# A graph network kernel: GpSimd waits once for each pair of edge groups, not for each group

## The chip, the cores and the metric

One core of a Trainium2 chip runs the whole kernel. The metric is the time of one execution on the device in microseconds (us). The kernel before was run three times: 3107.74, 3111.16 and 3117.75 us, with a median of 3111.16 us.

## What is computed

Four graph layers run over the same graph of 3125 nodes and 53125 directed edges; a layer's output is added to its input and normalised. Features are 128 wide, in float32.

```python
x = _layernorm(x + _L0_gnn_ref(x, edge_index, edge_type_4, ...), axis=-1)     # relation layer
x = _layernorm(x + _L1_gnn_ref(x, edge_index, edge_attr_64, ...), axis=-1)    # messages
x = _layernorm(x + _L2_gnn_ref(x, ..., node_type_3, src, dst), axis=-1)       # attention heads
x = _layernorm(x + _L3_gnn_ref(x, edge_weight, src, dst), axis=-1)            # weighted sum
```

The relation layer, for each of 4 relation types:

```python
rel_in = jnp.concatenate([node_features[src], node_features[tgt]], axis=1)
rel_t = _lrelu(rel_in @ W_R[r] + b_R[r])
...
e = _lrelu(jnp.concatenate([Q, K], axis=1) @ a_w + a_b)[:, 0]
attn = ex / jnp.maximum(denom[tgt], 1e-16)
h = h + jax.ops.segment_sum(V * attn[:, None], tgt, num_segments=num_nodes)
```

The attention layer computes a score for 8 heads of 16 features for every edge, a softmax over the edges of one destination, and a weighted sum. The last layer is `segment_sum(vals[:, None] * x[cols], rows)`: here the rows are the sources, while the edges lie in the order of their destinations.

## The kernel before

**Groups.** The edges are cut into Q = 104 groups of 512, a group into J = 4 tiles of 128 edges, one edge on each partition. Thirteen groups make a chunk of the softmax. Nodes are worked on in NG = 5 blocks of 640.

**Passes.** After tables are laid out (0 to 97 us of the trace), four passes go over the 104 groups, one behind the other: the relation pass (97 to 816 us), the message pass (935 to 1640 us), the head pass (1678 to 2325 us) and the scatter pass (2325 to 2968 us). A last pass over the nodes (2968 us to the end) reads what the scatter pass has written. The node work of a pass is woven into its later turns.

**Programs.** Each engine has its own program, written out as a list of turns; the engines meet at semaphores. `hold(engine, semaphore, n)` is a wait for the semaphore to reach n, and nothing when n is 0 or less.

**Relation pass.** In turn q, SyncE (`load`) brings the keys of the group (L710) and 4 small windows of the destination table (L715), for which it waits on `expanded` of two groups before and on `parted_keys`. ScalarE makes a one-hot `spread` of the keys (`spread_made`). TensorE (`expand`, L754) multiplies spread by window, so that each edge has its destination's row in PSUM (3 buffers), and counts `expanded`. GpSimd (`pool_program`, L690 to L697) gathers the source rows with one indirect DMA for each tile (L696) into one of GS = 6 buffers `gathered`. VectorE adds both (`join`, L988), applies the leaky ReLU (L992), and multiplies (L997); ScalarE sums (L897, `reduced`). TensorE adds up a group 21 turns later (L769 to L771).

**Head pass.** It has the same shape: loads L1899 and L1909, `expand` at L1955, gathers of 4 x 128 rows at L1867 into a ring of RING = 24 groups `kv`, `score` on VectorE (L2231, L2234), which reads them, and much later `weigh` (L2240, `weighed`), which frees the ring's slot. At the start of the pass SyncE also loads the links of the first chunk (L1891).

**Scatter pass.** `weigh_row(q)` (VectorE, L2169, `taken`) waits for `expanded` of its group and writes edge weight times node row into a slot of the same ring. `tag(q)` (ScalarE, L2106, `tagged`) adds a column with the source. `mark` and `place` (VectorE, L2176 to L2197, with TensorE's `count`, L1968 to L1970) find, for two groups at a time, in which row of `rows_by_src` each edge belongs (`placed`). GpSimd (`send_rows`) writes the rows with one indirect DMA for each tile (L1881). `number[True, q]` is the place of scatter group q in the order of expansions, and for the text below E(q) is the expansion of scatter group q. In this order `weigh_row(q)` waits for E(q), while `send_rows` before the change waits for E(q + 1) as well.

Instructions of one engine start in program order, so an unmet wait on GpSimd holds every indirect DMA behind it.

Of the kernel before, what the change touches and what calls it, by code (L numbers as in the profile page):

```python
# [32 lines left out]
Q = -(-E // GE)  # L33
# [21 lines left out]
RING = 2 * CH  # L55
# [11 lines left out]
def build(nc, x, src, dst, edge_attr_64, edge_type_4, edge_weight, node_type_3,  # L67
# [340 lines left out]
    def far_spread(eng, program):  # L408

        reach = nc.values_load(wide[0:1, 3:4], engines=[eng.engine], min_val=0, max_val=GE,  # L410
                               skip_runtime_bounds_check_because="every node has an edge of its own")
        with eng.If(reach < REACH):
            program(1, REACH, True)
        with eng.Else():
            program(GE // P, P, False)
# [6 lines left out]
    def hold(eng, semaphore, count):  # L422

        if not (isinstance(count, int) and count <= 0):
            eng.wait_ge(semaphore, count)
# [183 lines left out]
    def rel_layer(u_cols, agg, share, parts):  # L609

        with ExitStack() as ctx:
            tmp, psum, sem, pair = scope(ctx, "e0")
            GS, SLOTS, WS, KS, SS, AHEAD = 6, CH + 8, 3, 2, 2, CH + 8
# [50 lines left out]
            spread_made, expanded, joined, shaped, scaled, reduced = (sem(n) for n in  # L664
                ("spread_made", "expanded", "joined", "shaped", "scaled", "reduced"))
# [23 lines left out]

            def pool_program(pool):  # L690
                for q in range(Q):
                    hold(pool, reduced, q - GS + 1)
                    hold(pool, expanded, q)
                    pool.nop(nofuse=True)
                    for j in range(J):
                        pool.indirect_dma_start(gathered[:, q % GS, j, :], None, rel_table,  # L696
                                                bass.IndirectOffsetOnAxis(ap=rel_idx[:, q * J + j:q * J + j + 1], axis=0)).then_inc(src_in[q % GS], 16)  # L697
# [534 lines left out]
            with nc.Block() as block:  # L1232
                @block.gpsimd
                def _(pool):
                    pool_program(pool)

                @block.sync
                def _(sp):
                    tiles_and_spread(sp, lambda nw, early: sync_program(sp, nw, early))

                @block.tensor
                def _(pe):
                    tiles_and_spread(pe, lambda nw, early: pe_program(pe, nw, early))

                @block.scalar
                def _(act):
                    tiles_and_spread(act, lambda nw, early: act_program(act, nw, early))

                @block.vector
                def _(dve):  # L1250
                    tiles_and_spread(dve, lambda nw, early: dve_program(dve, nw, early))
# [462 lines left out]
    def head_and_rows(agg2, parts, below, bucket, first_bucket, bucket_base):  # L1714

        with ExitStack() as ctx:
            tmp, psum, sem, pair = scope(ctx, "e2")
            ROWS = CH * H
            RING, WS = 24, 3
# [70 lines left out]
            prepared, bucketed, scanned, carried, counted, chosen, ranked, placed, tagged, starts_mm, starts_out, based = (sem(n) for n in  # L1790
                ("prepared", "bucketed", "scanned", "carried", "counted", "chosen", "ranked", "placed", "tagged", "starts_mm", "starts_out", "based"))
            SAID, BASES = 4, 4 * (Q // PIECE)
            links_in = sem("links_in")
            distant, spread_made, expanded, taken, reduced, weighed, marked, marked_far, summed, parted, added = (sem(n) for n in
                ("distant", "spread_made", "expanded", "taken", "reduced", "weighed", "marked", "marked_far", "summed", "parted", "added"))
# [38 lines left out]
            def numbers(early):  # L1834

                return {which: n for n, which in enumerate(x for t in range(first_row(early) + Q) for x in expansions(t, early))}
# [23 lines left out]

            def pool_program(pool):
                for q in range(Q):
                    hold(pool, weighed, q - RING + 1)
                    hold(pool, expanded, q - 4)
                    pool.nop(nofuse=True)
                    for j in range(J):
                        pool.indirect_dma_start(kv[:, q % RING, j, :], None, kv_table,  # L1867
                                                bass.IndirectOffsetOnAxis(ap=src_idx[:, q * J + j:q * J + j + 1], axis=0)).then_inc(src_in[q % RING], 16)
                far_spread(pool, lambda nw, gw, early: send_rows(pool, early))

            def send_rows(pool, early):
                number = numbers(early)
                for q in range(Q):
                    slot = (Q + q) % RING
                    pool.wait_ge(taken, number[True, q] + 1)
                    pool.wait_ge(expanded, number[True, min(q + 1, Q - 1)] + 1)
                    pool.wait_ge(tagged, q + 1)
                    pool.wait_ge(placed, q // 2 + 1)
                    pool.nop(nofuse=True)
                    for j in range(J):  # L1880
                        pool.indirect_dma_start(in_order, bass.IndirectOffsetOnAxis(ap=row[:, q // 2 % RS, q % 2 * J + j:q % 2 * J + j + 1], axis=0),  # L1881
                                                kv[:, slot, j, 0:D + 1], None).then_inc(sent[slot], 16)
                for slot in range(RING):
                    pool.wait_ge(sent[slot], 16 * J * len([q for q in range(Q) if (Q + q) % RING == slot]))
# [641 lines left out]
            with nc.Block() as block:  # L2526
                @block.gpsimd
                def _(pool):
                    pool_program(pool)

                @block.sync
                def _(sp):
                    far_spread(sp, lambda nw, gw, early: sync_program(sp, nw, gw, early))

                @block.tensor
                def _(pe):
                    far_spread(pe, lambda nw, gw, early: pe_program(pe, nw, gw, early))

                @block.scalar
                def _(act):  # L2540
                    far_spread(act, lambda nw, gw, early: act_program(act, nw, gw, early))

                @block.vector
                def _(dve):
                    far_spread(dve, lambda nw, gw, early: dve_program(dve, nw, gw, early))
# [259 lines left out]
```

## Time and profile before

| what | us |
|---|---|
| median of three runs | 3111.16 |
| lowest and highest run | 3107.74 and 3117.75 |
| span of the profiled execution | 3116.5 |
| GpSimd busy in it | 1686.7 |
| TensorE busy in it | 2083.1 |
| VectorE busy in it | 1599.0 |
| ScalarE busy in it | 1173.8 |

The profile is of one execution of its own. Its span, from first to last instruction, is 3116.5 us, which is 5.3 us above the median of the runs; no other time is recorded for that execution. An engine's idle time in front of an instruction is shown with what ended it. "issue" stands for time in which the profile sees no other engine that released it; a wait that was put on a semaphore ahead of an instruction on GpSimd can be counted there. The ends of matmuls are modelled. The shares of busy time hide that the passes have different limits, so the stretches are read one by one.

### The profile page before, as it was taken

To read this page: it belongs to the slowest core of one execution; us is meant where nothing else is said; L and a number is where in the kernel's file an instruction comes from. 1 tells how busy PE (TensorE), PEld (TensorE's weight loads), DVE (VectorE), ACT (ScalarE), POOL (GpSimd) and SP (SyncE) were. 2 spreads that over 40 slices of the span, in tenths; PEclk is the share of its full clock that TensorE was granted. 3 is DMA by queue.
4 is the path that set the end of the run, shared out by engine and by line. 5 is a ranking of instruction groups with operands and counts; after the bars stand their busy time and mean duration, and the time that the engine had idled before them with its cause. 6 is when DMAs were issued, how large, how long until landed. Compare 5 with 4: busy or idle time off the path is not lost. (4 is left out here: it accounts for less than half of the span.)

```text
span 3116.5 us, 39457 instructions
## 1 busy us (share of the span) xinstructions
PE 2083.1 (67%) x9935; PEld 1681.0 (54%) x9935; DVE 1599.0 (51%) x4408; ACT 1173.8 (38%) x3329; POOL 1686.7 (54%) x1704
## 2 busy tenths in 40 slices
PE   5336787878764778888883356766776665455367
PEld 2235666766653666667662356565664443333267
DVE  4246767786751233423232334666687754544256
ACT  2245556555321223233231234454454322222144
POOL 3366656565105566656623666666646666666600
PEclk9655555556556899899995555555567775655589
DMA  6644434443103223232312444444432222222265
GB/s 222 233 140 130 129 107 135 121 128 113 37 9 99 65 70 81 71 82 66 83 51 72 125 119 121 120 121 119 128 100 65 77 78 69 73 70 71 65 198 178
DMA packets 244613, 322.43 MB, mean 103 GB/s; under 512 B 105346, under 2 KB 160931, under 8 KB 243045
## 3 DMA queue, kind: packets, MB, share of 16 engines
q0 software_dynamic: 66560, 163.90, 18.3%
q1 hardware_dynamic: 177797, 155.67, 16.6%
q8 instruction: 93, 1.52, 0.2%
q14 instruction: 163, 1.34, 0.1%
HBM read 257.60 MB, written 63.38 MB: 103 GB/s over the span
## 5 line engine op out<-in xcount | busy, mean ns | idle before, releaser
L1318 POOL DMA_INDIRECT e_gathered<-msg_src_table,src_idx x416 | 399.9, 961 | 393.7 <-POOLq L364 142.1
L696 POOL DMA_INDIRECT e_gathered<-rel_src_table,rel_idx x416 | 427.9, 1029 | 310.2 <-issue 256.3
L1867 POOL DMA_INDIRECT e_kv<-kv_table,src_idx x416 | 411.1, 988 | 302.8 <-issue 198.9
L1881 POOL DMA_INDIRECT rows_by_src<-e_kv,e_row x416 | 422.2, 1015 | 226.4 <-issue 193.5
L1955 PE MATMUL e_ps_q<-e_window,e_spread 64*128 64x128 f32 x1664 | 347.6, 374 | 145.4 <-issue 61.3
L1955 PEld LDWEIGHTS e_ps_q<-e_window,e_spread 64*128 64x128 f32 x1664 | 302.3, 271 | 218.6 <-issue 187.7
L2092 ACT ACTIVATE e_spread<-e_offsets,e_minus_lane 64x512 f32<-64x512 f32 x208 | 149.1, 717 | 576.0 <-remote 370.0
L754 PE MATMUL e_ps_r<-e_window,e_spread 64*128 64x128 f32 x832 | 205.5, 421 | 156.4 <-DMA e_window<-rel_dst_table 117.6
L754 PEld LDWEIGHTS e_ps_r<-e_window,e_spread 64*128 64x128 f32 x832 | 176.7, 311 | 182.9 <-DMA e_window<-rel_dst_table 126.0
L1991 PE MATMUL e_ps_a<-e_onehot,e_weighted 128*128 128x128 f32 (+1 forms) x832 | 184.3, 394 | 127.6 <-DVE e_weighted L2240 85.4
L1581 DVE TENSOR_TENSOR e_shifted<-e_ps_m,e_b 128x512 f32<-128x512 f32 x104 | 71.8, 690 | 344.6 <-remote 169.6
L1991 PEld LDWEIGHTS e_ps_a<-e_onehot,e_weighted 128*128 128x128 f32 x832 | 165.6, 296 | 153.2 <-DVE e_weighted L2240 99.3
L769 PE MATMUL e_ps_a<-e_typed,e_rel 128*128 128x128 f32 (+1 forms) x832 | 192.1, 407 | 48.2 <-DVE e_typed L1005 30.7
L1968 PE MATMUL e_ps_c<-e_inside,e_minus_after 128*128 128x392 f32 x104 | 77.1, 841 | 205.1 <-DVE e_carry L2185 76.6
L769 PEld LDWEIGHTS e_ps_a<-e_typed,e_rel 128*128 128x128 f32 x832 | 174.1, 309 | 69.7 <-DVE e_typed L1005 36.3
L1425 PE MATMUL e_ps_a<-e_mixed,e_message 128*128 128x64 f32 x832 | 113.8, 282 | 83.8 <-DVE agg L1590 60.3
L897 ACT ACTIVATE e_gathered<-e_gathered 128x128 f32<-128x128 f32 x416 | 122.8, 296 | 122.7 <-issue 70.3
L1409 PEld LDWEIGHTS e_ps_h<-ident,e_gathered 128*128 128x128 f32 x832 | 127.7, 220 | 60.5 <-issue 60.5
L2099 ACT ACTIVATE e_onehot<-marks,part_t 128x66 f32<-128x66 f32 x416 | 110.1, 335 | 123.7 <-remote 99.2
L1425 PEld LDWEIGHTS e_ps_a<-e_mixed,e_message 128*128 128x128 f32 x832 | 107.1, 201 | 90.6 <-issue 89.8
L1504 ACT ACTIVATE e_hidden<-e_ps_h,e_b 128x512 f32<-128x512 f32 x104 | 71.4, 687 | 222.6 <-remote 116.6
L1404 PE MATMUL e_ps_h<-e_rhs,e_lhs 128*128 128x512 f32 x208 | 128.5, 704 | 36.7 <-issue 24.3
(446 smaller groups left out, 4233.3 us busy)
## 6 DMA issues: line engine op xcount, KB each, us to landing
n_rows<-rows_by_src SPq DMA_DIRECT2D x26, 1032.0 KB
e_offsets<-group_offsets SPq DMA_DIRECT2D x208, 128.0 KB
e_keys<-tile_keys SPq DMA_DIRECT2D x104, 128.0 KB
e_window<-rel_dst_table SPq DMA_DIRECT2D x416, 32.0 KB
e_mixed<-in_edge_attr_dram SPq DMA_DIRECT2D x103, 128.0 KB
rel_src_table<-t_up SPq DMA_DIRECT2D x5, 2560.0 KB
e_gathered<-rel_src_table,rel_idx POOLq DMA_INDIRECT x416
e_gathered<-msg_src_table,src_idx POOLq DMA_INDIRECT x416
```

The source lines that it names most:

```text
L696: pool.indirect_dma_start(gathered[:, q % GS, j, :], None, rel_table, bass.IndirectOffsetOnAxis(ap=rel_idx[:, q * J + j:q * J + j + 1], ax ...
L754: mm = pe.matmul(ps_r[q % 3][:, j, :], spread[:, at % SS, j * P:(j + 1) * P], window[:, at % WS, j, :], start=(w == 0 and (nw == 1 or j == ...
L769: pe.matmul(ps_a[at % 2][:, a:b], rel[:, p % SLOTS, j, :], by_key[:, a:b], start=True, stop=True, skip_group_check=True)
L1318: pool.indirect_dma_start(gathered[:, q % GS, j, :], None, msg_table, bass.IndirectOffsetOnAxis(ap=src_idx[:, q * J + j:q * J + j + 1], ax ...
L1404: pe.matmul(ps_h[q % 2][:, :, :], lhs[0:k, at % WS, :], rhs[0:k, at % 2, :], start=(w == 0), stop=False, skip_group_check=True).then_inc(s ...
L1409: mm = pe.matmul(ps_h[q % 2][:, j, :], gathered[:, q % GS, j, :], ident[:, :], start=False, stop=True, skip_group_check=True)
L1425: mm = pe.matmul(ps_a[:, :], message[:, q % 2, j, :], picked, start=(j == 0), stop=(j == J - 1))
L1867: pool.indirect_dma_start(kv[:, q % RING, j, :], None, kv_table, bass.IndirectOffsetOnAxis(ap=src_idx[:, q * J + j:q * J + j + 1], axis=0) ...
L1881: pool.indirect_dma_start(in_order, bass.IndirectOffsetOnAxis(ap=row[:, q // 2 % RS, q % 2 * J + j:q % 2 * J + j + 1], axis=0), kv[:, slot ...
L1955: mm = pe.matmul(ps_q[n % 2][:, j, :], spread[0:gw, at % 2, j * P:(j + 1) * P], window[0:gw, at % WS, :], start=(w == 0 and (nw == 1 or j ...
L1991: mm = pe.matmul(to[:, 0:n], weighted[:, p % 2, j, :], wide_hot[:, j * (gw + 2):j * (gw + 2) + n], start=(j == 0), stop=(j == J - 1), skip ...
L2092: act.activation(spread[0:gw, at % 2, :], offsets[0:gw, n % WS, :], ACT.Abs, bias=minus_lane[0:gw, w:w + 1]).then_inc(distant, 1)
```

## The change

In the relation and head passes, GpSimd's two waits (and the empty instruction that carries them) stand ahead of even groups only. The first wait asks for one group more, since the eight DMAs behind it fill two buffers. The second, for `expanded`, keeps its even value, so odd groups start with no wait of their own. In the scatter pass the four waits also stand ahead of even groups only, and ask for what the odd group needed: `taken` and `tagged` of both groups, and E(q + 2) for an even q. The message pass is as before. The number of indirect DMAs, their order and their data are the same.

```diff
--- before.py
+++ after.py
@@ -689,9 +689,10 @@
 
             def pool_program(pool):
                 for q in range(Q):
-                    hold(pool, reduced, q - GS + 1)
-                    hold(pool, expanded, q)
-                    pool.nop(nofuse=True)
+                    if q % 2 == 0:
+                        hold(pool, reduced, q - GS + 2)
+                        hold(pool, expanded, q)
+                        pool.nop(nofuse=True)
                     for j in range(J):
                         pool.indirect_dma_start(gathered[:, q % GS, j, :], None, rel_table,
                                                 bass.IndirectOffsetOnAxis(ap=rel_idx[:, q * J + j:q * J + j + 1], axis=0)).then_inc(src_in[q % GS], 16)
@@ -1860,9 +1861,10 @@
 
             def pool_program(pool):
                 for q in range(Q):
-                    hold(pool, weighed, q - RING + 1)
-                    hold(pool, expanded, q - 4)
-                    pool.nop(nofuse=True)
+                    if q % 2 == 0:
+                        hold(pool, weighed, q - RING + 2)
+                        hold(pool, expanded, q - 4)
+                        pool.nop(nofuse=True)
                     for j in range(J):
                         pool.indirect_dma_start(kv[:, q % RING, j, :], None, kv_table,
                                                 bass.IndirectOffsetOnAxis(ap=src_idx[:, q * J + j:q * J + j + 1], axis=0)).then_inc(src_in[q % RING], 16)
@@ -1872,11 +1874,12 @@
                 number = numbers(early)
                 for q in range(Q):
                     slot = (Q + q) % RING
-                    pool.wait_ge(taken, number[True, q] + 1)
-                    pool.wait_ge(expanded, number[True, min(q + 1, Q - 1)] + 1)
-                    pool.wait_ge(tagged, q + 1)
-                    pool.wait_ge(placed, q // 2 + 1)
-                    pool.nop(nofuse=True)
+                    if q % 2 == 0:
+                        pool.wait_ge(taken, number[True, q + 1] + 1)
+                        pool.wait_ge(expanded, number[True, min(q + 2, Q - 1)] + 1)
+                        pool.wait_ge(tagged, q + 2)
+                        pool.wait_ge(placed, q // 2 + 1)
+                        pool.nop(nofuse=True)
                     for j in range(J):
                         pool.indirect_dma_start(in_order, bass.IndirectOffsetOnAxis(ap=row[:, q // 2 % RS, q % 2 * J + j:q % 2 * J + j + 1], axis=0),
                                                 kv[:, slot, j, 0:D + 1], None).then_inc(sent[slot], 16)
```

## Rows read from the trace of the kernel before

**Rows 1.** Busy us by stretch: PE, PEld, DVE, ACT, POOL; PEclk, DMA share.
```profile
97.00:816.00 719.00, 495.30 (x2128) 421.42 (x2129) 476.00 (x1445) 385.26 (x1528) 427.86 (x416) 0.54 0.44 127
...
2325.00:2968.00 643.00, 360.99 (x1323) 241.06 (x1321) 334.87 (x751) 178.28 (x415) 422.19 (x416) 0.64 0.24 71
...
106.00:250.00 144.00, 54.22 (x218) 46.25 (x218) 58.39 (x101) 61.40 (x232) 92.92 (x92) 0.50 0.50 142
```

**Rows 2.** The waits of GpSimd by line (us in total, times, longest us).
```profile
POOL e_gathered L696 <- issue: 256.3, 412, 5.9
POOL e_kv L1867 <- issue: 198.9, 406, 4.1
POOL rows_by_src L1881 <- issue: 193.5, 402, 4.0
```

**Rows 3.** The waits of all engines by line: VectorE for gathers, TensorE for windows.
```profile
PE e_ps_r L754 <- DMA e_window<-rel_dst_table: 117.6, 24, 21.8
...
DVE e_rel L988 <- DMA e_gathered<-rel_src_table,rel_idx: 47.2, 13, 5.9
```

**Rows 4.** The chain that ended last, where the last pass begins (start, us, what).
```profile
2972.61 5.18 DMA n_rows<-rows_by_src
```

**Rows 5.** Timeline of GpSimd, start of the relation pass (last: idle before).
```profile
110.15 0.95 POOL L696 DMA_INDIRECT e_gathered<-rel_src_table,rel_idx  x1 [0.30 <-issue]
118.00 0.94 POOL L696 DMA_INDIRECT e_gathered<-rel_src_table,rel_idx  x1 [6.90 <-PE e_ps_r L754]
...
137.24 0.94 POOL L696 DMA_INDIRECT e_gathered<-rel_src_table,rel_idx  x1 [3.62 <-PE e_ps_r L754]
```

**Rows 6.** Timeline of SyncE in that stretch, the loads of four windows.
```profile
118.12 2.45 SPq L715 DMA_DIRECT2D e_window<-rel_dst_table  x4
...
125.55 8.63 SPq L715 DMA_DIRECT2D e_window<-rel_dst_table  x4
```

**Rows 7.** Timeline of TensorE and VectorE in that stretch.
```profile
134.41 2.08 PE L754 MATMUL e_ps_r<-e_window,e_spread 64*128 64x128 f32 x8 [9.71 <-DMA e_window<-rel_dst_table]
...
136.52 0.69 DVE L988 TENSOR_TENSOR e_rel<-e_gathered,e_ps_r 128x512 f32<-128x512 f32 x1 [4.24 <-PE e_ps_r L754]
```

**Rows 8.** Timeline late in the relation pass: eight gathers, loads beside them.
```profile
663.29 0.94 POOL L696 DMA_INDIRECT e_gathered<-rel_src_table,rel_idx  x1 [1.37 <-issue]
...
672.54 0.95 POOL L696 DMA_INDIRECT e_gathered<-rel_src_table,rel_idx  x1 [0.30 <-issue]
...
668.55 6.99 SPq L715 DMA_DIRECT2D e_window<-rel_dst_table  x4
...
681.83 1.43 PE L754 MATMUL e_ps_r<-e_window,e_spread 64*128 64x128 f32 x5
```

**Rows 9.** Timeline at the start of the head pass, SyncE and VectorE.
```profile
1686.83 7.14 SPq L1891 DMA_DIRECT2D e_pen_c<-segment_gates  x8
...
1703.21 0.69 DVE L2231 TENSOR_TENSOR e_kv<-e_kv,e_ps_q 128x512 f32<-128x512 f32 x1 [11.90 <-remote]
```

**Rows 10.** Timeline of GpSimd, scatter pass: starts of runs of DMAs.
```profile
2602.15 1.36 POOL L1881 DMA_INDIRECT rows_by_src<-e_kv,e_row  x1 [3.43 <-issue]
...
2626.38 1.29 POOL L1881 DMA_INDIRECT rows_by_src<-e_kv,e_row  x1 [3.36 <-issue]
...
2812.51 1.08 POOL L1881 DMA_INDIRECT rows_by_src<-e_kv,e_row  x1 [1.82 <-issue]
...
2836.90 1.09 POOL L1881 DMA_INDIRECT rows_by_src<-e_kv,e_row  x1 [1.69 <-issue]
```

**Rows 11.** Timeline at the end of the scatter pass, VectorE and GpSimd.
```profile
2908.66 0.69 DVE L2169 TENSOR_TENSOR e_kv<-e_ps_q,w_t 128x512 f32<-128x512 f32 x1 [2.29 <-remote]
...
2909.38 0.97 POOL L1881 DMA_INDIRECT rows_by_src<-e_kv,e_row  x1 [0.97 <-issue]
...
2916.84 0.96 POOL L1881 DMA_INDIRECT rows_by_src<-e_kv,e_row  x1 [2.67 <-issue]
...
2956.32 0.97 POOL L1881 DMA_INDIRECT rows_by_src<-e_kv,e_row  x1 [0.30 <-issue]
```

## Prediction

> **What bounds the kernel now.** I first read the busy time by stretch. No engine is full in any pass that the change touches: the relation pass lasts 719 us with TensorE busy 495, VectorE 476 and GpSimd 428, and the scatter pass lasts 643 us with GpSimd busy 422 and TensorE 361 [rows 1]. So a pass is set by waits between engines, and what counts is who waits for GpSimd.
>
> Next come the waits by line. GpSimd's own idle time is large: 256, 199 and 194 us in the three changed lines [rows 2]. It doesn't matter by itself. It matters where somebody waits for the DMAs behind it. In the relation pass VectorE's join waits for gathers 13 times, 47.2 us in all, while TensorE waits for its windows 24 times, 117.6 us [rows 3]. In the head pass the view shows VectorE's score waiting for a gather once, and in the scatter pass nobody waits inside the pass for a row that was written. At its end somebody does: the chain that ended last goes through the load of those rows at 2972.61 [rows 4], which can't begin before the last write.
>
> Then the timelines. A gather takes 0.95 us, and behind one whose wait is already met 0.30 us pass, between groups as within them. A wait that binds costs more: group 0's last gather starts at 110.15, and group 1's first only at 118.00, after 6.90 us for its expansion [rows 5]. In the stretch from 106 to 250 us (groups 0 to 23) nothing is left to do from earlier groups; GpSimd is busy for 92.9 of 144 us there, TensorE for 54 [rows 1]. Here the gathers are close to the bound. Later a gather has usually landed some microseconds before its join.
>
> One more reading decides much of what follows. SyncE's load of four windows takes 2.45 us at 118.12, when GpSimd has just started, but 8.63 us at 125.55, when GpSimd has issued DMAs back to back since 118.00 [rows 6]. TensorE's multiplication waits 9.71 us for that load, the join behind it starts at 136.52, and GpSimd itself then starts at 137.24, 3.62 us idle, for the expansion before it [rows 7, 5]. Late in the relation pass it is the same: GpSimd issues eight gathers in a row from 663.29 to 673.5, and the load at 668.55 takes 6.99 us [rows 8]. At the start of the head pass, with a longer run of gathers, a load of eight small pieces takes 7.14 us, and a score comes 11.90 us after VectorE's last work [rows 9]. So a long run of indirect DMAs is not free for the others.
>
> **The change part by part.**
>
> *The waits taken away that were met already.* Fifty-two waits of a pass fewer, each worth nothing: the gap behind a met wait is the same 0.30 us as within a group [rows 5]. Term: 0.
>
> *Relation pass, the opening.* Odd groups lose their wait for their own expansion. Group 1 then starts at about 111.4 (110.15 + 0.95 + 0.30) in place of 118.00, 6.6 us earlier. The other odd waits before group 24 add up by my reading of the same timeline to about 6, so 13 us is the most that the opening can give, if each gather is the last thing its join waits for. It gives nothing if windows come last. Group 1 is gathered earlier, but groups 2 and 3 then form a run of eight as before, and the window of group 3 is loaded beside it, as now at 125.55; that load, not a gather, holds the join at 136.52 [rows 6, 7]. What GpSimd gains ahead of that point is taken back there. I take -3, nearer to the window's row; bounds -13 and 0.
>
> *Relation pass, the rest.* Idle ahead of L696 put to "issue" is 256.3 us over 412 gathers [rows 2]; 412 x 0.30 = 123.6 is the plain gap, so 132.7 us stand at binding boundaries. The two shown in the rows are 3.62 and 1.37 [rows 5, 8], 2.2 above the gap in the mean, hence some 60 boundaries, half of them odd. So about 30 times two runs of four gathers (5 us) become one of eight (10 us). The odd gather comes earlier, for a join that mostly has another input last; but the load of windows that falls into the second half of the run can take 6.99 or 8.63 us instead of 2.45. The load at 668.55 ended at 675.54 and was used only at 681.83 [rows 8], 6.3 us later: it cost nothing. The one at 125.55 cost what it was late. Bounds: below 0; above, one in four of 30 pairs with the whole 6.2 us (8.63 - 2.45), 46 us. I take +4, two thirds of one such load, because after the opening SyncE is as a rule a group ahead.
>
> *Relation pass, the tighter wait for `reduced`.* It asks for q - 4 rather than q - 5; the expansion of q waits for the join of q - 3, a group later in VectorE's order, and ScalarE's sum of q - 4 follows its own join by a few us. It is met before the other wait. Term 0; above, one ScalarE group late on occasion, inside the +46.
>
> *Head pass.* Gathers are far ahead of the score (the ring has 24 groups, and only once does a score wait for one), and GpSimd already runs in long stretches. Neither the slot asked for earlier nor the odd gathers' earlier start meets anybody. If that cover were gone, the even group would wait one VectorE turn, some 5 us. The long run at its start [rows 9] has no binding odd wait in it and stays. Term 0, bounds 0 and +5.
>
> *Scatter pass, the body.* Odd groups' waits stay as they were in substance; even groups wait one expansion and one `weigh_row` longer. What matters is whether lumps of eight slow the pass. The trace has both forms: in runs of sixteen DMAs, four groups take 2626.38 - 2602.15 = 24.23 us; in runs of four to eight, 2836.90 - 2812.51 = 24.39 us [rows 10]. The pace is the same, so it is set by TensorE and VectorE, not by how GpSimd is fed. The slots, 24 groups, and the six pairs of row numbers hide the delay of one group. Term 0.
>
> *Scatter pass, the end.* Here there is no cover. Group 95 starts at 2909.38, 0.72 us after VectorE takes up expansion 96 at 2908.66; group 96 at 2916.84 after 2.67 us idle, and from there 32 writes run back to back to 2956.32 + 0.97 [rows 11]. With the pair, groups 94 and 95 both wait for that expansion: they start at 2909.4, eight writes take 8 x 1.27 = 10.2 us and 0.3 for a first one that is longer, and group 96 starts at 2919.9. That is 3.1 us later, and each write behind it, and the load of the last pass that waits for them all. Bounds: 0, if 96's own wait moves earlier, and +5.1, a whole group; I take +3.
>
> *A rule beside the rows.* By the rows, a window load beside a run of gathers goes from 2.45 to 8.63 us [rows 6]. The Trainium skill (DMA: Bandwidth & Descriptors, section "Issuing engines are not separate DMA queues") says that DMAs started by different engines run on the same 16 DMA engines and interleave, and that issuing from several saves only issue time. By it, lumping the same gathers would cost SyncE no more than its share of the same engines, and the +4 would be 0; the trace disagrees, since SyncE's issue itself is stretched.
>
> *The sum.* 0 - 3 + 4 + 0 + 0 + 3 = +4 us on the span of 3116.5, 3120.5 us. The median of the runs stands at 0.9983 of that span (3111.16 / 3116.5), so 3115 us.
>
> **The rivals.**
>
> *The opening decides, faster.* The 47.2 us that VectorE waited for gathers [rows 3] are mostly in the opening, and 6.9 us of it come from one odd wait [rows 5]. If the gathers are what bounds groups 0 to 23, and SyncE gets its loads out before a run grows long, all 13 us return: 3116.5 - 13 + 3 = 3106.5, or 3101 as a median, and more if the same holds in later places (another 10: 3091). Against it is the join at 136.52, bound by a window.
>
> *Longer runs starve the window loads, slower.* If one in eight of the 30 new runs of eight puts its full 6.2 us on TensorE, that is +23; with the tail's 3 and no gain in the opening, 3142.5, or 3137 as a median. It decides once four or so of those loads come late. For it: TensorE already waits 117.6 us for windows [rows 3], and 8.63 us is measured. Against: the load of 6.99 us that hurt nobody [rows 8].
>
> *Nothing of it is felt.* Each expansion is due before GpSimd gets there, or the joins have another input last: 0 everywhere but the tail, and that too may be taken by the work that goes on beside it. 3111.
>
> **How the numbers follow.** My forecast (a few us) has a chance of 0.32 and no effect 0.10, together 0.42 for within 0.3%, about 9 us, which is what a measurement of this kernel can tell from no change. Faster has 0.26: two shown places speak for it, one against. Slower has 0.32: it has many places in which to happen, and the tail's sign is certain. The range is 3090 (the opening's gain and more) to 3138 (one load in eight late); beyond it I leave 0.2, mostly above. The likeliest case's own range is 3105 to 3122.
>
> **What the profile after would show.** The step on the opening is right if group 1's gathers start near 111 and the join of group 3 is still held by a window; wrong if VectorE's waits for gathers fall by 10 us or more and the pass ends earlier. The step on the rest is right if TensorE's waits for windows stay near 118 us, and wrong if they grow by 20 or more while loads of 6 to 9 us multiply. In the scatter pass the pace should stay at 24.2 to 24.4 us for four groups, and the distance from `weigh_row` of group 96 to the last write should grow from 48.6 us (2908.66 to 2957.29) to about 52. What would make it wrong most easily: that the start of one pass moves, by chance, into another pattern of runs, since several patterns stand side by side in this trace, and each turn's start depends on the one before.

## The result, and the profile after

The changed kernel takes 3154.78 us (median of 4 runs, 3149.52 to 3165.36), the kernel before 3109.45 us (4 runs) beside it. The ratio is 1.0134, with a 95% interval of 1.0105 to 1.0163: 1.3% slower, some 42 us, where I had forecast a span 4 us longer.

The profiled execution has a span of 3157.5 us, 41.0 above the one before. The busy time by stretch, for the relation, head and scatter passes of the changed kernel (columns as in [rows 1]):

```profile
97.00:841.00 744.00, 488.39 (x2139) 414.63 (x2139) 478.17 (x1449) 386.86 (x1534) 425.66 (x416) 0.55 0.42 123
...
1705.00:2339.00 634.00, 375.75 (x1576) 324.20 (x1576) 338.77 (x803) 265.36 (x644) 408.35 (x416) 0.54 0.42 120
...
2368.00:3000.00 632.00, 346.35 (x1286) 231.79 (x1285) 327.74 (x735) 172.57 (x399) 425.57 (x416) 0.65 0.24 71
```

From the first indirect DMA of one pass to that of the next, which I worked out from the starts in the timelines, the relation pass with its node turns and the way to the message pass took 861.7 us in place of 837.1, the message pass 737.3 in place of 737.6, the head pass 662.7 in place of 648.9, and the writes of the scatter pass 629.4 in place of 626.5. Of the head pass's 13.8 us, 3.9 lie between its first gather and the end of its last (631.7 in place of 627.8); the other 9.9 lie in the wait ahead of the first write, which is 31.0 us in place of 21.1. No engine is busy for longer over the whole execution than before by more than 0.5 us, so the loss is made of waits.

The waits by line, of the changed kernel (us in total, times, longest):

```profile
POOL e_gathered L697 <- issue: 282.2, 413, 13.7
...
PE e_ps_r L755 <- DMA e_window<-rel_dst_table: 85.6, 19, 22.4
...
POOL rows_by_src L1884 <- DVE e_kv L2172: 80.5, 15, 31.0
...
DVE e_rel L989 <- DMA e_gathered<-rel_src_table,rel_idx: 41.7, 14, 5.5
```

and, of the kernel before, the wait ahead of the first write:

```profile
POOL rows_by_src L1881 <- DVE e_row L2197: 21.1, 1, 21.1
```

Against [rows 2, 3], VectorE's waits for gathers fell by 5.5 us and TensorE's for windows by 32. Neither is the place of the loss. GpSimd's longest wait in the relation pass went from 5.9 to 13.7 us. In the scatter pass 80.5 us of its idle time are now put to VectorE, but that is mostly another name for waits that stood under "issue" before: all its idle time there rose from 226.4 to 235.8 us, by no more than the wait ahead of the first write did. In the relation pass the thirty odd waits that had bound are gone, with 71 us of idle time in them, while the idle time at even groups rose from 68 to 157 us (both beyond the plain gaps). GpSimd comes sooner and is held longer, since the engines that feed it are late. To see why, one has to go to a long wait.

The opening of the relation pass in the changed kernel, GpSimd, SyncE and VectorE:

```profile
112.30 0.94 POOL L697 DMA_INDIRECT e_gathered<-rel_src_table,rel_idx  x1 [0.30 <-issue]
...
123.32 0.94 POOL L697 DMA_INDIRECT e_gathered<-rel_src_table,rel_idx  x1 [6.31 <-PE e_ps_r L755]
...
126.72 2.46 SPq L716 DMA_DIRECT2D e_window<-rel_dst_table  x4
...
130.44 4.41 SPq L716 DMA_DIRECT2D e_window<-rel_dst_table  x4
...
118.83 0.69 DVE L989 TENSOR_TENSOR e_rel<-e_gathered,e_ps_r 128x512 f32<-128x512 f32 x1 [9.25 <-PE e_ps_r L755]
...
135.27 0.69 DVE L989 TENSOR_TENSOR e_rel<-e_gathered,e_ps_r 128x512 f32<-128x512 f32 x1 [2.68 <-DMA e_gathered<-rel_src_table,rel_idx]
```

Group 1 is now gathered from 112.30, its join came earlier, and the join of group 3 at 135.27 is 1.3 us earlier than at 136.52 [rows 7], and waits for its gather and not, as I had it, for a window. Up to group 18 nearly all joins lie ahead of their times before, by up to 3.8 us, and the next ten lie on either side. That is about the gain of 3 us that I had put down. From about group 29 on the pass falls back, 10 us behind by group 44, and 24 by group 76, in steps. One step, in which group 67 loses 10 us:

```profile
550.35 0.94 POOL L697 DMA_INDIRECT e_gathered<-rel_src_table,rel_idx  x1 [2.11 <-issue]
...
569.75 0.95 POOL L697 DMA_INDIRECT e_gathered<-rel_src_table,rel_idx  x1 [0.31 <-issue]
584.41 1.15 POOL L697 DMA_INDIRECT e_gathered<-rel_src_table,rel_idx  x1 [13.71 <-issue]
...
552.19 5.26 SPq L716 DMA_DIRECT2D e_window<-rel_dst_table  x4
...
561.12 10.03 SPq L716 DMA_DIRECT2D e_window<-rel_dst_table  x4
...
577.69 2.45 SPq L716 DMA_DIRECT2D e_window<-rel_dst_table  x4
...
555.42 1.98 PE L770 MATMUL e_ps_a<-e_typed,e_rel 128*128 128x128 f32 x8
...
564.79 0.37 PE L770 MATMUL e_ps_a<-e_typed,e_rel 128*128 128x128 f32 x1 [1.18 <-issue]
566.95 0.37 PE L770 MATMUL e_ps_a<-e_typed,e_rel 128*128 128x128 f32 x1 [1.79 <-issue]
569.05 0.37 PE L770 MATMUL e_ps_a<-e_typed,e_rel 128*128 128x128 f32 x1 [1.73 <-issue]
571.19 0.37 PE L770 MATMUL e_ps_a<-e_typed,e_rel 128*128 128x128 f32 x1 [1.76 <-issue]
...
573.51 0.69 DVE L989 TENSOR_TENSOR e_rel<-e_gathered,e_ps_r 128x512 f32<-128x512 f32 x1 [11.21 <-remote]
```

GpSimd starts at 550.35 and issues sixteen gathers without a break, to 570.7: two pairs have run together. The load of four windows at 552.19 takes 5.26 us, the next one at 561.12 10.03 us, the first one after the run 3.34, and the second 2.45 again. TensorE shows the same: its pieces of work stood eight in 1.98 us at 555.42, but from 564.79 to 571.19 one matmul starts every 2.1 us, with nothing named that it waits for ("issue"). VectorE gets its expansion after 11.21 us, when the run is over, and GpSimd has then to wait 13.71 us itself. That a long run stretches a load beside it I had seen [rows 6, 8, 9]; that TensorE's own instructions crawl as well I had not priced.

### The profile page after: what moved, and what is told of

It is laid out like the page before. It is cut to its first block and busy times, and to the rows that moved or that the text cites. A ratio compares the mean times of both kernels' runs of the same rounds, so it can differ in the third digit from the quotient of the medians.

```text
span 3157.5 us, 39251 instructions
## 1 busy us (share of the span) xinstructions
PE 2060.7 (65%) x9935; PEld 1666.1 (53%) x9935; DVE 1598.8 (51%) x4408; ACT 1174.3 (37%) x3329; POOL 1683.6 (53%) x1704
## 5 line engine op out<-in xcount | busy, mean ns | idle before, releaser
L1884 POOL DMA_INDIRECT rows_by_src<-e_kv,e_row x416 | 425.6, 1023 | 235.8 <-issue 144.8
L1958 PE MATMUL e_ps_q<-e_window,e_spread 64*128 64x128 f32 x1664 | 336.0, 367 | 130.3 <-issue 61.5
L1958 PEld LDWEIGHTS e_ps_q<-e_window,e_spread 64*128 64x128 f32 x1664 | 294.5, 266 | 200.2 <-issue 182.4
L1405 PE MATMUL e_ps_h<-e_rhs,e_lhs 128*128 128x512 f32 x208 | 131.6, 719 | 42.5 <-issue 24.2
L989 DVE TENSOR_TENSOR e_rel<-e_gathered,e_ps_r 128x512 f32<-128x512 f32 x104 | 70.9, 682 | 172.0 <-remote 54.1
```

Of the source, the lines that this page charges most:

```text
L1405: pe.matmul(ps_h[q % 2][:, :, :], lhs[0:k, at % WS, :], rhs[0:k, at % 2, :], start=(w == 0), stop=False, skip_group_check=True).then_inc(s ...
L1958: mm = pe.matmul(ps_q[n % 2][:, j, :], spread[0:gw, at % 2, j * P:(j + 1) * P], window[0:gw, at % WS, :], start=(w == 0 and (nw == 1 or j ...
```

## The experiments

All ratios are to the kernel before on the same chip. In this section "theory A" is that unbroken runs of GpSimd's indirect DMAs stretch the other engines' instructions, that is, make them take longer, and that the change makes such runs longer. A run is counted as unbroken while no gap in it is over 0.5 us. The first four ran together.

**One pass at a time.** Relation pass alone:

```diff
                 for q in range(Q):
-                    hold(pool, reduced, q - GS + 1)
-                    hold(pool, expanded, q)
-                    pool.nop(nofuse=True)
+                    if q % 2 == 0:
+                        hold(pool, reduced, q - GS + 2)
+                        hold(pool, expanded, q)
+                        pool.nop(nofuse=True)
```

> The waits in pairs in the relation pass alone; head and scatter passes as before. Theory A (runs of eight and sixteen gathers stretch SyncE's window loads and TensorE's instructions, and the relation pass carries most of the loss): 20 to 30 us slower than before, the message pass starting 20 to 27 us later. Theory B (the loss is spread over the passes as a shift of patterns): under 10 us slower.

The same with the diff's head part alone, and with its scatter part alone:

> The waits in pairs in the head pass alone. Theory A: 0 to 10 us slower, since GpSimd runs long there with either form. Theory B, and that the tighter slot or the lumps matter in the head pass: 10 to 20 us slower, with the scatter pass starting later by as much.

> The waits in pairs in the scatter pass alone. Prediction: pace unchanged and the last write 3 us later relative to the last expansions, so 3 us slower. Theory C (the first pair waits for an expansion that comes late, as the scatter pass started 10 us later in the changed kernel's trace): 8 to 15 us slower.

Measured: 1.0075 (1.0047 to 1.0103) for the relation pass, 1.0039 (1.0019 to 1.0060) for the head pass, 1.0048 (1.0024 to 1.0072) for the scatter pass. On a median of 3138.54 us that is 24, 12 and 15 us. Each part costs by itself, and the three add up to 1.6%, which the intervals allow beside 1.34%. The head pass cost more than the 5 us that the prediction allowed it at most, and more than the 10 us that theory A did here; the scatter pass cost five times the 3 us that I gave it, which is theory C's band of 8 to 15. For the relation pass the 24 us lie in theory A's band, but its second sign didn't show: the message pass started at 958.4 us, against 951.2 to 954.4 in the other three traces of this chip, and not 20 to 27 us later. (Its profiled execution is one of its faster ones, 3150.18 us beside a median of 3163.79.)

Theory C's late first pair is there, but it isn't the cost. From the end of the last gather to the first write it is 26.3 us in the trace with the scatter pass in pairs and 21 to 25 us in traces with the head and scatter passes as before. It is 26.0 us as well in the version "late, but not in a lump" below, which isn't slower.

**The run broken, all else kept.** GpSimd fills a small buffer ahead of each odd group:

```diff
                     if q % 2 == 0:
...
+                    else:
+                        for i in range(3):
+                            hold(pool, rested, q // 2 * 3 + i)
+                            pool.memset(rest[:, :], 0.0).then_inc(rested, 1)
+                        pool.wait_ge(rested, q // 2 * 3 + 3)
+                        pool.nop(nofuse=True)
```

> The relation pass in pairs, but ahead of each odd group GpSimd fills a small buffer three times (each waiting for the one before), so that eight gathers are never issued back to back; other passes as before. The fills compute nothing. Theory A: the loss of the relation pass goes, 0 to 8 us slower than before. Theory B, or that the tighter wait or the earlier odd gathers do it: as slow as with the relation pass in pairs alone, within 5 us.

Its GpSimd timeline at a group boundary:

```profile
302.22 1.09 POOL L704 DMA_INDIRECT e_gathered<-rel_src_table,rel_idx  x1 [0.30 <-issue]
303.31 0.74 POOL L700 MEMSET e_rest<- 128x128 f32 x3
304.81 1.92 POOL L704 DMA_INDIRECT e_gathered<-rel_src_table,rel_idx  x1 [0.75 <-issue]
```

The gap between the last gather of one group and the first of the next is 1.50 us (304.81 - 303.31) in place of 0.30, and 1.49 to 1.66 at all 52 odd groups; the odd group still starts without its old wait, and the even one has the tighter wait for `reduced`. Measured: 1.0002 (0.9980 to 1.0024), against 1.0075 without the rest on the same chip. The loss is gone, though GpSimd needs 1.2 us more for each pair. So the moved wait costs nothing. The rest does two things at once, it breaks the run and it brings the odd gathers 1.2 us later, and this run doesn't part the two; that the break is what helps is read from SyncE's loads further below.

**The rest in all three passes** (in the head and scatter passes one fill, a gap of 0.9 us), on another chip with the next three:

> The changed kernel with a rest of GpSimd ahead of each odd group in all three passes: three fills of a small buffer in the relation pass (the gap grows from 0.30 to 1.8 us there), one fill in the head and scatter passes (a gap of about 1 us). The fills compute nothing. Theory A (unbroken runs of indirect DMAs do the harm, in all three passes): within 8 us of before. Theory D (in head and scatter the lump of eight or the later even group does it, not the unbroken run): 15 to 30 us slower than before, as the two passes cost alone.

Measured 1.0038 (1.0012 to 1.0063), 12 us, which lies between theory A's band and theory D's, with an interval that reaches into both. It is less than the changed kernel in both its measurements (1.0134, and 1.0107 with an interval of 1.0069 to 1.0145 below), so most of the loss comes back, not all. The remainder isn't a matter of run length: with the rests no run in the three passes is longer than eight DMAs, where the kernel before has runs of up to 32. From the first gather of the head pass to the first write, its trace has 653.9 us, against 662.7 to 667.6 in the three traces with that pass in pairs without a rest, and 643.4 to 657.4 in the nine with it as before. In its trace the last write starts 64.6 us after `weigh_row` 96, in that of before 47.7; the four rests in that stretch explain some 2 us of it, and the remainder isn't traced.

**Late, but not in a lump.** In the scatter pass each group keeps a wait, for one group more:

```diff
-                    pool.wait_ge(taken, number[True, q] + 1)
-                    pool.wait_ge(expanded, number[True, min(q + 1, Q - 1)] + 1)
-                    pool.wait_ge(tagged, q + 1)
+                    pool.wait_ge(taken, number[True, min(q + 1, Q - 1)] + 1)
+                    pool.wait_ge(expanded, number[True, min(q + 2, Q - 1)] + 1)
+                    pool.wait_ge(tagged, min(q + 2, Q))
```

> Scatter pass only: every group keeps a wait of its own, but asks for one group more (weigh_row and tag of q + 1, E(q + 2)), so that writes are as late as the even ones of the pairs and are not lumped. Theory A: the lumps cost, so only the tail's 3 to 6 us remain. Theory E (the later even group costs, since it holds ring slots and row numbers longer, or since the last writes come later): 10 to 18 us slower.

Measured 1.0003 (0.9981 to 1.0024). The later wait of the even groups, the one price that I had put into the scatter pass, costs nothing that can be measured; 3 us would lie inside the interval. What is left for the 0.48% of the scatter pass in pairs is the lump of eight. That is by elimination, and between two chips: the two intervals meet at 1.0024.

**More breaks than before.** The kernel before with one fill ahead of odd groups in the head and scatter passes:

> The kernel before, with one fill of a small buffer on GpSimd ahead of odd groups in the head and scatter passes, which breaks its runs of 16 to 32 DMAs. Theory A: since the kernel before has such runs itself, 5 to 20 us faster. Rival: TensorE and VectorE set the pace there, and the longer GpSimd turn eats what is won; within 0.3%.

Measured 1.0007 (0.9986 to 1.0027). No run was longer than eight DMAs there, and nothing was won: theory A missed as far as it said that all long runs cost. The head and scatter passes of before live with the runs that they have.

**The dose.** One wait for four groups in the relation pass:

```diff
+                    if q % 4 == 0:
+                        hold(pool, reduced, q - GS + 4)
+                        hold(pool, expanded, q)
+                        pool.nop(nofuse=True)
```

> Relation pass only: one wait ahead of sixteen gathers, for four groups. Theory A: the longer the run, the longer window loads are stretched: at least 45 us slower, twice the loss of the pairs. Theory B (a pattern, not a dose): about the same 20 to 25 us, or less.

Measured 1.0436 (1.0408 to 1.0464), 136 us. Its timelines of GpSimd, SyncE and VectorE show a run of sixteen:

```profile
402.95 1.13 POOL L697 DMA_INDIRECT e_gathered<-rel_src_table,rel_idx  x1 [9.65 <-PE e_ps_r L755]
...
432.93 0.95 POOL L697 DMA_INDIRECT e_gathered<-rel_src_table,rel_idx  x1 [9.71 <-ACT e_gathered L898]
...
408.87 6.56 SPq L716 DMA_DIRECT2D e_window<-rel_dst_table  x4
...
422.62 0.69 DVE L989 TENSOR_TENSOR e_rel<-e_gathered,e_ps_r 128x512 f32<-128x512 f32 x1 [14.18 <-remote]
```

The run goes from 402.95 to 423.2, the load at 408.87 takes 6.56 us, and a join comes after 14.18 us. There are 22 such runs of sixteen in this pass, in place of two. GpSimd then waits for a buffer, which the group before frees late, so the trace alone can't tell the run from the buffers. For that the rest was put in again, in two sets of runs.

**A set on a chip that doesn't stretch.** Four more kernels went to one chip together:

> Relation pass only: one wait for four groups as in the run that was 4.4% slower, with three fills of a small buffer on GpSimd ahead of the second, third and fourth group, so that no more than four gathers are issued without a break. The fills compute nothing. Theory A (unbroken runs): at least two thirds of the 136 us come back, 0 to 45 us slower than before. Theory F (buffers: four groups wait for a buffer that is freed late): 90 us or more slower.

> Relation pass only, in pairs, but the odd group keeps an instruction that waits for what the even one has waited for already, so the wait is met. Theory A: a met wait leaves the 0.30 us gap and breaks nothing, so 20 to 28 us slower, as the pairs alone. Rival: the wait instruction itself is a break; within 0.3% of before.

> Relation pass only, in pairs, with one small fill ahead of odd groups in place of three: a gap of about 1 us instead of 1.8. Theory A, if any true pause ends the stretching: within 0.3% of before. If the pause must be long: 10 to 20 us slower.

> Scatter pass only, in pairs, with one small fill ahead of odd groups below 95. Theory A: of the 15 us that pairs cost there alone, at most the tail's 3 us remain. Theory D (the lump of eight or the later even group): 10 to 18 us slower.

There the kernel before took 2720.06 us, 13% less than on the others, and none of the four expectations had such a chip in view. The four came out at 1.0191 (1.0171 to 1.0211), 0.9993 (0.9983 to 1.0004), 1.0020 (1.0009 to 1.0031) and 1.0109 (1.0090 to 1.0127). The kernel with met waits, which issues in pairs in the relation pass, was to be 20 to 28 us slower and was not slower at all. Its busy time in the message, head and scatter passes, the start of the run of 192 gathers in its relation pass, and a load of SyncE beside it:

```profile
870.00:1402.00 532.00, 481.70 (x3271) 406.50 (x3271) 210.21 (x635) 203.76 (x376) 404.30 (x416) 0.95 0.37 94
1462.00:1998.00 536.00, 391.60 (x1664) 334.38 (x1664) 359.44 (x850) 278.80 (x674) 407.99 (x416) 0.57 0.51 144
2001.00:2551.00 550.00, 352.06 (x1302) 237.69 (x1301) 327.39 (x742) 173.93 (x407) 422.43 (x416) 0.68 0.28 82
...
121.00 0.94 POOL L696 DMA_INDIRECT e_gathered<-rel_src_table,rel_idx  x1 [5.64 <-PE e_ps_r L754]
...
195.93 2.45 SPq L715 DMA_DIRECT2D e_window<-rel_dst_table  x4
```

GpSimd is never idle beyond the gap of 0.30 or 0.31 us in these three passes: 416 DMAs in one run each, in 532, 536 and 550 us, where the same stretches, first to last DMA, are 652, 628 and 627 us long in the profile of the kernel before. The load at 195.93 lies 75 us into a run of 192 gathers, and takes 2.45 us; none of the 104 loads is over 3.61 us. So on this chip long runs don't stretch the loads, and there the pairs of the relation pass cost nothing. That agrees with theory A, but it isn't a clean removal of its cause: the chips differ in more than that. The message pass, whose runs are nearly all of four and eight where the kernel takes 3110 us, is from its first gather to the head pass's 738 us there and 593 here, the largest difference of all passes. A rest in the scatter pass costs here about what it takes, since GpSimd is the bound: 47 rests of 0.58 us are 27 us, and 30 were measured. In the relation pass it costs less: 52 such rests, 30 us, cost 5.

**The same again where it stretches.** The set was repeated, with the changed kernel beside it, and fell on a chip where the kernel before takes 3116.51 us:

> The changed kernel as it is, beside its own single parts on one chip. If SyncE's instructions are stretched beside long runs on this chip (a kernel before of some 3110 us): 1.0% to 1.6% slower. If they are not (a kernel before of some 2720 us): theory A says that pairs then cost nothing in the relation pass, and in the others GpSimd never pauses, so within 0.3%; a theory in which the wait itself does harm says 1% slower on either chip.

> The relation pass in pairs with a met wait ahead of odd groups, as before. On a chip with stretching: theory A 0.5% to 1.0% slower, as the pairs alone; if a met wait is a break, within 0.3%. On one without: within 0.2%.

```diff
-                    hold(pool, reduced, q - GS + 1)
-                    hold(pool, expanded, q)
+                    hold(pool, reduced, q - q % 2 - GS + 2)
+                    hold(pool, expanded, q - q % 2)
```

> One wait for four groups in the relation pass, with three fills ahead of each of the other three. On a chip with stretching: theory A 0 to 45 us slower in place of 136; theory F (buffers) 90 us or more. On one without: again some 50 us slower (1.9%).

```diff
+                    if q % 4 == 0:
...
+                    else:
+                        n = 3 * (q - q // 4 - 1)
+                        for i in range(3):
+                            hold(pool, rested, n + i)
+                            pool.memset(rest[:, :], 0.0).then_inc(rested, 1)
+                        pool.wait_ge(rested, n + 3)
+                        pool.nop(nofuse=True)
```

> The scatter pass in pairs with one fill ahead of odd groups below 95. On a chip with stretching: theory A at most 0.2% slower in place of 0.5%; theory D 0.4% or more. On one without: again 1.1% slower, since there GpSimd has no idle time in that pass to cover a rest.

Measured: the changed kernel 1.0107 (1.0069 to 1.0145); met waits 1.0058 (1.0031 to 1.0085), so a met wait is no break; four groups to a wait with rests 1.0011 (0.9989 to 1.0032), where without rests it was 1.0436; the scatter pass in pairs with a rest 1.0011 (0.9988 to 1.0034), where without it was 1.0048. The third is the strongest: the waits for buffers are asked for as without rests, and all 136 us are gone, within the interval (on another chip than the 136 us, but one with nearly the same time before). For the scatter pass the two intervals just overlap, so its rest is likely, not settled.

SyncE's loads tie these runs together. Counted from the timelines of the relation pass, of 104 loads of four windows:

| relation pass | loads over 6 us | all loads, us |
|---|---|---|
| four groups to a wait, with rests | 1 | 315 |
| pairs, with rests | 8 | 369 |
| kernel before | 12 | 391 |
| changed kernel, two traces | 16 and 17 | 398 and 423 |
| four groups to a wait | 26 | 443 |
| six kernels on the two chips without stretching | 0 | 262 to 264 |

The loads follow the length of the runs, shorter than before as well as longer. The time of the kernel follows only upward: fewer stretched loads than the kernel before has gained nothing.

**Rests everywhere.** Ahead of every group in all four passes of the kernel before, and in the first two:

> The kernel before with its waits as they were, and one small fill on GpSimd ahead of every group in all four passes, so that no run is longer than four DMAs (about 5 us), at some 0.75 us for each group. The fills compute nothing. Theory A, and that the stretching sets the pace of the kernel before on such chips too (a chip without it takes 390 us less): 20 us or more faster, if the chip stretches. Rival: the pace there is set by something else in those chips; within 0.5%, and slower by about 70 us on a chip without stretching, where GpSimd bounds three passes.

> The same in the relation and message passes alone. Theory A as for all passes: 10 us or more faster on a chip with stretching. Rival: within 0.5%.

Both fell on a chip without stretching (before: 2722.81 us) and measured 1.0712 (1.0697 to 1.0726) and 1.0304 (1.0289 to 1.0319). I had expected some 70 us for the first. It is 195 us for 416 rests, 0.47 us each. In the message, head and scatter passes, where GpSimd is the bound there, they last 55 to 65 us longer than in the trace with met waits, 0.53 to 0.62 us for each rest, close to the 0.58 us by which the gap grows. Whether breaking every run pays on a chip that stretches stays open. No version ran that beats the kernel before.

## Why the prediction was wrong

*Met waits cost nothing:* right, and more than that: a met wait in an odd group's place leaves the loss as it is, within the intervals (1.0058 beside 1.0075), and the gap stays 0.30 us.

*The opening, -3:* right in sign and size by the joins of groups 3 to 18 in this trace, but that may be luck: in the second trace of the changed kernel, on another chip, the joins are behind the times of before from group 8 on, by 7 us at group 14. That a window would still hold group 3 was wrong. The run in [rows 6] that I called eight gathers is one of twelve, from 118.00 to 133.6.

*Relation pass, the rest, +4:* this is the term that failed by most. The mechanism was right, the size was off: 24 us alone. That 30 odd waits bind, drawn from two rows of which one isn't even put to "issue", is so in the trace, by luck. I priced a new long run by SyncE's load only, and took it to be hidden by SyncE's lead in nearly all cases. The runs showed TensorE's matmuls at 2.1 us each too, and that pairs run together into sixteens (five runs of 15 or 16 and one of 24 in this trace, two of 16 before), where one cost 10 us. The count of window loads over 6 us rose only from 12 to 16 of 104, and their sum from 391 to 398 us, so the loads as such were never the whole price. The sign that I had named for this step was blind to it: TensorE's waits for windows were to grow by 20 us or more if it was wrong, and they fell by 32.

*Head pass, 0 to +5:* 12 us alone. I looked for someone who waits for a gather or a slot, found none, and put the odd waits at nothing. They weren't nothing: in the trace before, 18 odd waits bind in this pass, with 51 us of idle time in them, and each cuts a run. Without them the runs of sixteen DMAs or more went from 9 to 15. The zero for who waits for GpSimd holds (nobody waits for a gather in the changed trace), so the cost is likely in what its runs do to the engines beside it. A rest in this pass alone wasn't tried; that it is the run here as well rests on the kernel with rests in all three, and stays argued.

*Scatter pass, the body, 0:* by the pass alone this step failed, 15 us (8 to 23) where the tail was to cost 3. From the same pace in runs of sixteen and of four [rows 10] I read that lumps are harmless. They were the wrong comparison: the change turns few fours into sixteens, it joins sixteens into 24s (14 runs of sixteen and none of 24 before, 6 and 7 after). The pace, four groups in the mean of the whole pass, was 24.15 us before and 24.67 with this pass in pairs alone; in the changed kernel it is 24.27, within what I had said, so there the loss is hardly to be seen in this pass. GpSimd, TensorE and VectorE of the changed kernel in such a stretch:

```profile
2581.63 1.47 POOL L1884 DMA_INDIRECT rows_by_src<-e_kv,e_row  x1 [5.71 <-DVE e_kv L2172]
...
2606.62 1.47 POOL L1884 DMA_INDIRECT rows_by_src<-e_kv,e_row  x1 [4.24 <-DVE e_kv L2172]
...
2592.63 2.05 PE L1958 MATMUL e_ps_q<-e_window,e_spread 64*128 64x128 f32 x16
...
2605.15 0.69 DVE L2172 TENSOR_TENSOR e_kv<-e_ps_q,w_t 128x512 f32<-128x512 f32 x1 [4.74 <-remote]
```

The run from 2581.63 ends at 2602.4. TensorE's expansion is shown from 2592.63, VectorE can take it at 2605.15 only, and four groups take 24.99 us in place of 24.2. TensorE's end is modelled: by its record the expansion was done 10 us before anybody got it. That matmul ends are estimated, not observed, is also what the Trainium skill says (Perfetto Trace Analysis, section "Tensor Engine Instruction (MATMUL, LD_WEIGHTS)"); this row agrees. Whether TensorE itself was late or one of its windows, the trace doesn't show.

*The tail, +3:* VectorE and GpSimd at the end of the changed kernel's scatter pass:

```profile
2946.38 0.69 DVE L2172 TENSOR_TENSOR e_kv<-e_ps_q,w_t 128x512 f32<-128x512 f32 x1
...
2968.12 1.29 DVE L2172 TENSOR_TENSOR e_kv<-e_ps_q,w_t 128x512 f32<-128x512 f32 x2 [7.49 <-remote]
...
2955.39 0.97 POOL L1884 DMA_INDIRECT rows_by_src<-e_kv,e_row  x1 [0.81 <-issue]
...
2968.84 0.97 POOL L1884 DMA_INDIRECT rows_by_src<-e_kv,e_row  x1 [3.54 <-issue]
...
2998.19 0.97 POOL L1884 DMA_INDIRECT rows_by_src<-e_kv,e_row  x1 [0.30 <-issue]
```

From `weigh_row` 96 to the end of the last write it is 2999.16 - 2946.38 = 52.8 us; I had said about 52, from 48.6 [rows 11]. It came another way, though: pair 96 was nearly on time (2955.39, 0.81 us idle), and pair 98 waited 3.54 us. Kernels whose scatter pass is as before show 48 to 55 us to the start of the last write in their traces, and this one 51.8, so one trace doesn't prove the size, and that 52.8 met my 52 is luck as far as can be told.

The rival "longer runs starve the window loads" named the cause and had 3137 us; it was too cheap in the relation pass and blind to the other two. And the terms for the head and scatter passes, and with them the range, came only from who waits for whom.

## What to carry to other kernels

A wait that often binds may do good that no view credits to it: in the relation pass it cut GpSimd's indirect DMAs mostly into runs of four and eight, and the other engines caught up in the gaps. Before taking waits away, list the run lengths of the engine that they hold, and look at what the neighbours' same instruction takes early and late in a run. And test on more than one chip: pairs in the relation pass, with a met wait, cost 0.6% on one and nothing on another. The whole change wasn't run on a chip of the second kind.

## What the runs showed of the hardware

On four of six sets of runs the kernel before took 3109 to 3139 us; in the other two, 2720 and 2723. In the slower ones, SyncE's instructions (DMA issues and register moves) grow to about 0.7 us each in long runs of GpSimd's indirect DMAs. In the relation pass of the kernel before, 79 of 187 of them last 0.66 to 0.80 us once a run is older than 7 us, and 54 of 895 in its first 7 us; in the scatter pass it is 11 of 105 beyond 7 us. On a faster chip (the kernel with met waits) it is none of 1434 in the relation pass, and no load takes more than 3.61 us, though one run is 192 gathers long. TensorE's matmuls start every 2.1 us in the run at 550.35 of the changed kernel. GpSimd's own DMAs mostly take 0.94 to 0.97 us in both. For VectorE no instruction is shown to grow; it waits. What differs between those chips no run shows, and neither does a mechanism for the stretching. Long runs don't explain all of the 390 us between them either: on a slower chip, breaking the runs of the head and scatter passes into fours and eights won nothing (1.0007).
